# Two-layer graph attention: loading a row group of the adjacency in one transfer instead of four

## What is computed

```python
h = jnp.maximum(_layernorm(x, axis=-1), 0.0)
x = x + _L0_gnn_ref(h, adj, L0_gnn_W, L0_gnn_b_W, L0_gnn_a_vec, L0_gnn_b_a)
h = jnp.maximum(_layernorm(x, axis=-1), 0.0)
x = x + _L1_gnn_ref(h, adj, L1_gnn_W_w, L1_gnn_W_b, L1_gnn_a)
# a layer, in short:
Wh = h @ W + b
e = leaky_relu((Wh @ a1)[:, None] + (Wh @ a2)[None, :], 0.2)
attention = softmax(where(adj > 0, e, -9e15), axis=1)
return attention @ Wh
```

## Time and profile before

| | us |
|---|---|
| median of 3 runs | 2206.73 |
| lowest and highest of the 3 | 2205.22, 2226.64 |
| profiled execution | 2236.48 |
| its span, first to last instruction | 2234.6 |

### The profile page before, as it was taken

How to read it: one execution, slowest core, us unless ns; L and a number is a source line. 1 busy time by engine, 2 the same in 40 slices (tenths; PEclk the granted TensorE clock), 3 DMA queues, 4 the chain that set the end, 5 groups by cost and what they waited for, 6 DMA issues and landing times.

```text
span 2234.6 us, 49031 instructions
## 1 busy us (share of the span) xinstructions
PE 2001.2 (90%) x16866; PEld 1698.2 (76%) x16866; DVE 1773.5 (79%) x2733; ACT 1139.9 (51%) x1097; POOL 318.6 (14%) x496
## 2 busy tenths in 40 slices
PE   5456889999988888899888879999999999999998
PEld 3234678887777777788777768888888888888887
DVE  6565778997777777789877678888888888888884
ACT  4455667886667677777777332222333333222331
POOL 6440112322111112222112300000000000000000
PEclk9997999999999999999999989999999999999999
DMA  5659999999999999999999650000000000000000
GB/s 140 167 138 231 258 273 297 339 277 271 269 265 256 259 269 275 283 303 286 279 271 277 176 108 29 28 28 28 28 27 27 28 28 28 28 28 28 28 28 9
DMA packets 117077, 357.46 MB, mean 160 GB/s; under 512 B 24624, under 2 KB 74032, under 8 KB 80176
## 3 DMA queue, kind: packets, MB, share of 16 engines
q1 hardware_dynamic: 114736, 340.23, 57.5%
q10 hardware_dynamic: 2304, 16.78, 1.9%
HBM read 314.84 MB, written 42.07 MB: 160 GB/s over the span
## 4 chain that ended last, share of the span: by engine, by line
PE 46%; DMA 37%; ACT 6%; SPq 4%; issue 3%; DVE 3%; DVEq 0%; POOL 0%; ACTq 0%; POOLq 0%
PE acc L541 45%; DMA adj_sb<-in_adj_dram 34%; ACT sign_a L603 5%; SPq L254 3%; DMA node_rows<-row_parts 2%; DMA mask_bytes<-pair_a 1%; DVE ext L793 0%; DVE masks L865 0%; ACT row_parts L591 0%; DMA masks<-in_x_dram 0%; PE ps_h L493 0%; SPq L280 0%; DVE row_parts L800 0%; DVE stats L713 0%; DVE centred L726 0%
## 5 line engine op out<-in xcount | busy, mean ns | idle before, releaser
L541 PE MATMUL acc<-node_rows,masks 128*128 128x258 f16 x16384 | 1888.4, 276 | 71.8 <-DVE masks L872 69.5
L541 PEld LDWEIGHTS acc<-node_rows,masks 128*128 128x128 fp8e4 x16384 | 1615.5, 99 | 325.6 <-issue 79.4
L603 ACT ACTIVATE sign_a<-adj_sb 128x2048 int8<-128x2048 int32 x256 | 489.1, 1910 | 285.0 <-DMA adj_sb<-in_adj_dram 284.2
L616 ACT ACTIVATE sign_z<-t_row,neg_s 128x2048 int8<-128x2048 f32 x256 | 504.4, 1996 | 2.0 <-DVE masks L865 1.9
L622 ACT ACTIVATE part_a<-acc,coef_a 128x258 f32<-128x258 f32 x128 | 60.2, 471 | 677.6 <-PE acc L541 677.6
L812 DVE TENSOR_SCALAR sign_z<-t_row,neg_s 128x2048 int8<-128x2048 f32 x256 | 326.9, 1278 | 2.9 <-issue 2.4
L872 DVE TENSOR_SCALAR masks<-masks 128x2048 uint32<-128x2048 uint32 x256 | 311.6, 1217 | 0.3
L865 DVE STREAM_TRANSPOSE masks<-sign_z 128x2048 uint32<-128x2048 uint32 x128 | 294.9, 2304 | 0.1
L892 DVE SCALAR_TENSOR_TENSOR part_ac<-acc,coef_c,part_a 128x258 f32<-128x258 f32 x128 | 61.9, 484 | 238.3 <-ACT part_a L622 238.3
L438 POOL TENSOR_TENSOR h_sum<-h_sum,ext 128x128 f32<-128x128 f32 x126 | 113.2, 898 | 736.9 <-DVE ext L793 733.3
L493 PE MATMUL ps_h<-w_ext,centred_t 128*128 128x133 f32 x256 | 80.9, 409 | 119.1 <-ACT centred_t L578 115.6
(11 more groups left out here) (83 smaller groups left out, 612.9 us busy)
## 6 DMA issues: line engine op xcount, KB each, us to landing
adj_sb<-in_adj_dram SPq DMA_DIRECT2D x1024, 256.0 KB, 11.1
node_rows<-row_parts SPq DMA_DIRECT2D x128, 129.0 KB, 9.2
node_rows<-node_rows SPq DMA_DIRECT2D x32, 516.0 KB, 12.3
mask_bytes<-pair_a ACTq DMA_DIRECT2D x16, 1024.0 KB, 10.8
pair_a<-mask_bytes SPq DMA_DIRECT2D x16, 1024.0 KB, 4.8
x_old<-in_x_dram SPq DMA_DIRECT2D x64, 64.0 KB, 12.6
x_after_layer<-x_new SPq DMA_DIRECT2D x64, 64.0 KB, 13.1
x_old<-x_after_layer SPq DMA_DIRECT2D x64, 64.0 KB, 1.8
```

What stands on the lines that cost most here:

```text
L541: mm = pe.matmul(acc[T.p][s][:, 0:ROW], stationary[s][:, c // BYTES, c % BYTES, :], node_rows[:, c, ROW * s:ROW * (s + 1)], start=(c == 0) ...
L603: nc.scalar.activation(sign_a[:, T.p, SPAN * r:SPAN * (r + 1)], adj_sb[:, r, :], ACT.Sign, scale=-1.0) \
L616: nc.scalar.activation(sign_z[:, T.p, SPAN * r:SPAN * (r + 1)], t_row[:], ACT.Sign, scale=-1.0, bias=neg_s[:, ds(RGROUPS * T.t + r, 1)]).t ...
```

## The change

`load_adj` issues one transfer of 1 MB instead of four of 256 KB. The destination is all 128 partitions of the row group. The source is the same 32 rows, read in the order quadrant, row, column: the slowest dimension has the 4 quadrants, the next the 32 rows, and the last the 2048 columns. The bytes and their places are the same, and so is each contiguous run, 2048 int32 or 8 KB. The semaphore's target at L602 falls from 64 to 16 for each tile. The list of quadrants in the order 0, 2, 1, 3 goes.

```diff
-QUAD_ORDER = (0, 2, 1, 3)
@@ block.sync
             def load_adj(T, r):
-                for a in QUAD_ORDER:
-                    sp.nop(nofuse=True)
-                    sp.dma_start(adj_sb[QROWS * a:QROWS * (a + 1), r, :],
-                                 adj[ds(T.t * TILE + QROWS * r, QROWS), SPAN * a:SPAN * (a + 1)]) \
-                      .then_inc(adj_loaded[r], 16)
+                sp.nop(nofuse=True)
+                sp.dma_start(adj_sb[:, r, :],
+                             adj[ds(T.t * TILE + QROWS * r, QROWS), :].rearrange("i (a c) -> a i c", a=QUADS)) \
+                  .then_inc(adj_loaded[r], 16)
@@ block.scalar, cast
-                act.wait_ge(adj_loaded[r], 16 * QUADS * (T.t + 1))
+                act.wait_ge(adj_loaded[r], 16 * (T.t + 1))
```

## The result

| | us |
|---|---|
| before, median of 4 runs (lowest, highest) | 2214.66 (2205.22, 2226.64) |
| after, median of 4 runs (lowest, highest) | 3800.38 (3798.04, 3807.92) |
| after, span of the profiled execution | 3799.8 |
| ratio after to before, 95% interval | 1.716, 1.706 to 1.727 |

The changed kernel is slower by 72%.

The account below looks back on a forecast made before the run. The prediction took layer 0 to be bound by the adjacency's arrival. It summed 2236 - 1080 + 4225 (four engines) + 30 (node stage) = 5411 us, and with the median 30 us lower forecast 5380 us, range 3650 to 6400.

Parts of the forecast that it names:

- What bounds the kernel: Layer 0 set by how fast the adjacency comes in, 1080 us for 63 tiles; layer 1 bound by PE, 910 us.
- the node stage: Before layer 0: stored rows queue behind tile 0's row groups on four engines, 30 us more, ends 0 and 60.
- SP's fewer issues: Adjacency loads: one issue instead of four saves up to 1.3 us a row group, worth nothing while engines are full.
- the wait: At L602: counting to 16 for a tile instead of 64 is the same event, worth nothing.
- the casts: ACT's casts of the row groups, and all later work, stay unchanged: worth nothing.
- Four engines: Adjacency loads: dealt out along the four quadrants, so 4 of 16 engines carry them, 12 idle; 84 in 100.
- The time of a run: Layer 0: one 8 KB run takes an engine 0.508 us, so 67.1 us a tile, 4225 us for 63 tiles.
- the ceiling: Layer 0: always two engines on one way in, 0.620 us a run, 81.8 us a tile, 5156 us.
- the first rival: Layer 0: four engines hardly sharing a way in, 0.31 to 0.40 us a run, 3700 to 4480 us; 36 in 100.
- The stretch in the kernel before: Layer 0: runs stretched by 1.6, read as two engines sharing a way into the partitions, not an HBM limit.
- The clock: PE in layer 0: 14.6 us a tile, about 29 at half clock, far less than the loads take.

Follow-up runs that it names:

- e4_four_of_four: Kernel before, its four 256 KB transfers onto 32 partitions read so that the source's slowest dimension has 4 parts instead of 32: 3770 us.
- e10_eight: Kernel before, its four 256 KB transfers onto 32 partitions read so that the source's slowest dimension has 8 parts: 2506 us, ratio 1.147.
- e2_contig: Changed kernel, one 1 MB transfer a row group, source read in the order it lies, slowest dimension 128 parts: 2094 us.
- e3_pitch: Changed kernel, one 1 MB transfer reading 128 rows, a quarter of the columns, its 128 parts 32 KB apart: 2099 us.
- e1_halves: Changed kernel, each row group loaded in two 512 KB transfers onto 64 partitions, source's slowest dimension 2: 6307 us.
- e5_contig_quads: Kernel before, its four 256 KB transfers onto 32 partitions each reading 256 KB that lie in one piece: ratio to before 1.004.
- e6_order_0123: Kernel before, quadrants loaded in the order 0, 1, 2, 3 instead of 0, 2, 1, 3: ratio to before 1.048.
- e7: Kernel before, layer 0 loads split over two queues, SP issuing quadrants 0 and 1, ACT 2 and 3: ratio to before 1.054.
- e8: Kernel before, layer 0 loads split over two queues, SP issuing quadrants 0 and 2, ACT 1 and 3: ratio to before 1.067.
- e9_first_tile_only: Kernel before, only tile 0's four row groups, loaded in the node stage, in the changed form: median 2290 us against 2209.

## Why the prediction was right, and where it was not

**What bounds the kernel: right.** Layer 0 was set by the arrival of the adjacency, layer 1 by PE. The whole difference lies in the former and in the node stage.

**SP's fewer issues, the wait, the casts: right, nothing.** An unexpected thing came on top: SP's issue takes 3.5 us at the median and up to 17 now. What holds it up, no run here tries by itself. In layer 0 it costs nothing, as the four engines never ran dry (38 us chain on 38 us). In the node stage it does cost something, see below.

**Four engines: right, and now shown.** The prediction took this end from the code, at 84 in 100. e4_four_of_four and e10_eight are the kernel before with nothing changed but the parts outside: 32, 8 and 4 give 2208, 2506 and 3770 us. Over all forms, with 2, 4, 8 and 128 parts, the times are 6307, 3770 to 3800, 2506 and 2094 us, at DMA shares of 0.14, 0.28, 0.54 and 0.90. So with 2, 4 and 8 parts outside as many engines carry the adjacency, and 16 with 128 (and with the 32 of the kernel before, at 1.02). Which of the 16 they are was not shown. One transfer of 1 MB on 128 partitions is fast only where both sides have such an outer dimension: 2094 us when they have, 3800 when not.

**The time of a run: wrong, and this is the term that was mis-sized.** The step took 0.508 us, the stretch that the earlier trace rows show for 16 engines on 32 partitions, taken between the 0.310 of an engine alone and twice that. No run shows that value for four engines over the layer; the trace gives 41.0 us a tile for 132 runs, 0.310 us. With that value the sum stood in the prediction as 3724 us. Of the 1580 us by which 5380 was too high, 4225 - 2584 = 1641 come from it; the node stage gives 35 back, and 30 more come back because the prediction took the median to lie 30 us below the profiled run, as in the kernel before, where here it lies 1 us below (3800.4 and 3801.6). So the range was met because it was wide enough to hold both values of this term, and not because the likeliest one was near. What happened can be seen in windows of the changed kernel behind the start of layer 0, with the columns of the earlier trace rows:

```profile
238.00:243.00 5.00, 2.25 (x11) 1.64 (x12) 4.85 (x4) 0.00 (x0) 0.00 (x0) 0.50 0.25 59
248.00:253.00 5.00, 5.00 (x47) 4.38 (x45) 0.00 (x0) 0.00 (x0) 0.00 (x0) 1.00 0.25 79
260.00:290.00 30.00, 0.00 (x0) 0.00 (x0) 0.49 (x1) 9.51 (x5) 0.00 (x0) 0.50 0.25 106
```

Four engines' worth is busy throughout (share 0.25), but moves 59 GB/s at first and 106 after some 20 us: 59/16/0.25 = 14.8 GB/s, 0.555 us a run, then 26.5 GB/s, 0.309 us.

What the engines do in that time can be seen in 4 us of each, in 40 slices of 0.1 us, where 82 GB/s is one 8 KB run that lands. The changed kernel from 238 us, the same from 270 us, and e4_four_of_four from 222 us:

```profile
GB/s 0 0 0 0 246 82 0 0 0 0 246 82 0 0 246 82 0 0 0 0 246 82 0 0 0 0 164 164 0 0 0 0 82 246 0 82 82 164 0 0
```
```profile
GB/s 82 82 164 82 82 164 82 82 164 82 82 164 82 82 164 82 82 164 82 82 164 82 82 82 82 164 82 82 82 82 164 82 82 164 82 82 164 82 82 164
```
```profile
GB/s 328 0 0 328 0 0 164 164 0 0 328 0 0 328 0 0 328 0 0 328 0 0 328 0 0 328 0 0 328 0 0 328 0 0 328 0 0 328 0 0
```

At first four runs mostly land within 0.2 us of each other, the next four 0.4 or 0.6 us after them. From 270 us a run or two land in every slice, four in 0.3 us or a little more. In e4_four_of_four four runs mostly land in one slice of 0.1 us, and the next four 0.3 us later. So landing together does not go with the slow pace in e4_four_of_four (107 GB/s), and does in the changed kernel (59 GB/s). By the code the two differ in where the four parts of a transfer go, a quadrant each or 8 partitions each in one quadrant, and in how far apart their sources lie, 8 KB in one row or 32 KB; neither spacing stretched 16 engines like that (0.367 us a run in e2_contig, 0.366 in e3_pitch). That leaves the partitions, as the author reads it; which engine writes which partition at a time is in no view, and no run shows it. The sum over all four engines is 59 GB/s there, against the 210 that one quadrant took the earlier trace rows, so a limit of a quadrant as a whole can't be the only cause. e1_halves has the same slow start with two engines, 34 GB/s.

So the slow pace was real, 0.555 us against the 0.620 that the prediction estimated as the ceiling, and it ended by itself. It did not come back: from 285 us to the end of layer 0 the slices of the page have 107 to 123 GB/s, and 400 to 2700 us has 116 at a share of 0.28, 0.316 us a run. The prediction weighed the first rival (0.31 to 0.40 us a run) at 36 in 100 and the stretch of the kernel before at 48, and took a state that lasts 20 us for one that lasts. What ends it was not shown.

**The stretch in the kernel before: right about the side, the rest not shown.** It was put down to two engines sharing a way into the partitions and not to the HBM or the pitch. e3_pitch (326 GB/s at the same pitch) and e5_contig_quads (1.004 of the time before, from a source in one piece) exclude the source. e10_eight has 0.319 us a run on the same 32 partitions with half the engines, and e6_order_0123 0.538 against 0.486 by the order of the quadrants alone. So the stretch goes with 16 engines on 32 partitions, and with which quadrants follow each other. That there is a way in that two engines share, and which partitions it serves, was the author's reading, and no run shows it. Why the stretch of the kernel before lasts, where the slow pace of the changed kernel ends after some 20 us, stays open too: two queues did not end it in e7 and e8, and it varies (0.39 us a run in the window at 401 us of the earlier trace rows, 0.508 at 701).

**The node stage: too small.** 30 us were put, with ends 0 and 60; it was 64.7. The place was right, as e9_first_tile_only shows: the four loads of tile 0 in the new form alone move the start of layer 0 by 64.6 us. Of the chain of the changed kernel from 40 to 240 us, the waits that answer:

```profile
58.81 30.79 DMA node_rows<-row_parts
123.69 28.82 DMA node_rows<-row_parts
173.88 33.15 DMA node_rows<-row_parts
```

They were 13.1, 15.5 and 13.9 us: 50 us of the 65 are in these three. The rest is SP itself, which the prediction left out. The chain goes through its reloads of the quadrants (line 278, 280 before), 0.43 us each before; after the second group of steps two of them took:

```profile
108.95 4.89 SPq L278
113.89 6.16 SPq L278
```

The twelve reloads ahead of the three waits take 21 us of the chain instead of 5. e4_four_of_four, whose four engines are at full pace at the start of layer 0, has three waits of 25.3, 26.2 and 24.5 us, and its layer 0 starts at 204.3 us, 41.6 us later than in the kernel before. So by the author's estimate some 42 us are the price of four engines at full pace, and some 23 us more that of the slow pace (the number of transfers differs too, and no window of the node stage has the adjacency alone to show its pace there). So the price of a transfer that holds a few engines was paid by the waits for stored rows: 25 to 33 us each in these two kernels, 13 to 15 before.

**The clock.** PE idles through more than half of layer 0 and its granted clock fell to a mean of 0.73 there, with 0.50 in the window of 260 to 290 us where it did nothing. The tile's 128 matmuls take some 19 us at this mean (1086 us for 7357 of them) and stay below the 41 us, so it costs nothing, as was put.

## What to carry to other kernels

Look at both sides of a transfer before making it larger: what counts is the slowest dimension that is left when it is issued, and here one of 4 instead of 32 left 12 of 16 engines without this work, at equal bytes, equal runs and a quarter of the issues. A DMA share that falls to 0.25 while the chain still waits for transfers is the sign of it. Where several transfers have to be made because the layout wants it, keep a slowest dimension of 32 or 128 parts in each, which kept all 16 engines busy here, where 2, 4 and 8 did not (no other number was tried), and take the quadrants in the order 0, 2, 1, 3: in the order 0, 1, 2, 3 the kernel took 4.8% longer.

## What the runs showed of the hardware that was not expected

- The four engines of the changed kernel began layer 0 slowly and came to full pace within some 20 us, and it stayed: 59 GB/s, then 106, and 116 with the other traffic from 400 to 2700 us; with two engines (e1_halves) 34, then 53 GB/s.
- Runs of four engines that land within 0.1 us of each other can still come at full pace: 107 GB/s in e4_four_of_four, whose four parts go to 8 partitions each of one quadrant.
- With 16 engines on 128 partitions (e2_contig) a busy engine moves 321/16/0.90 = 22.3 GB/s, 0.367 us a run, over a long stretch, where a lone mask load has 0.310. With four or eight engines it is 0.309 to 0.319. It did not matter, since PE was the bound; its cause was not tried.
- An issue on SP takes 0.316 us at the median in the kernel before, and 3.5 us, up to 17.2, in the changed one. The shortest issue differs with the form of the transfer as well: it takes 0.53 us with 4 (0.62 in e4_four_of_four) and 0.67 with 8, where e2_contig with 128 has 0.33.
- The time of the kernel before is not steady: its runs went from 2173 to 2253 us beside e9_first_tile_only and e10_eight, and its pace inside one layer 0 from 0.39 to 0.51 us a run. That the one comes from the other is likely, but not shown.
